# Attention in a macaron block: projections moved to nearly every second step, copies of turned blocks all on ScalarE

## The chip, the cores and the metric

The kernel runs on one core of a Trainium2 chip. The metric is the device time of one execution in microseconds (us). The core has TensorE (PE in the profile; its weight loads are the row PEld), VectorE (DVE), ScalarE (ACT), GpSimd (POOL) and SyncE (SP), which issues the DMAs. Each engine runs its own instructions in order and waits on semaphores for the others.

## What is computed

The block is half a gated feed-forward layer, an attention layer, and the half feed-forward layer again, each on the normalised input and added to it. There are 8 batch items of 512 tokens, width 512, 16 heads of 32 that share one key and one value head.

```
x = x + 0.5 * ffn(layernorm(x))       # silu(x wg) * (x wu), 2 of 4 kept, times wd
x = x + attn(layernorm(x))
x = x + 0.5 * ffn(layernorm(x))

attn: q = x wq', k, v = split(x wkv')        # rotary with xpos scales on q and k
      a = softmax(where(causal, -max, q k' / 32))
      out = (a v) wproj' + b
```

All of it is float32; a product of two float32 matrices is made of three products of rounded parts (high by high, low by high, high by low).

## The kernel before, and what sets the order of its work

The two feed-forward phases take about 1,080 us each; nothing of the change lies in them. Between them stands the attention phase, written by hand: `attention_phase` gives each engine a function `step(K)`, and the order of the calls in it is the order in which the engine works. There are 8 batches (B = 0 to 7) of 16 steps (k = 0 to 15), 128 steps K in all. Four steps make a group: one group of 4 heads, one tile of 128 queries in each step. `ORDER = (3, 0, 1, 2)` says that the first step of a group handles the long row (512 keys), and the next three handle rows of 128, 256 and 384 keys.

**What TensorE does in step K.** It turns (transposes) the probabilities of row K into one PSUM bank for each block of 128 keys (`turn_probs`, L1236): none for the long row, which goes through DRAM, and 1, 2 and 3 blocks for the others. It does the projection that a table sets at this step (`project`): 12 matmuls of 128x512 for keys and values (L1179), for the queries of a group of heads of the next batch (L1204), or for the output of 128 tokens of the batch before (L1267). In the fourth step of a group it turns the inverse sums (L1212), in some steps a normalised tile (L344). In the first step of a group it weighs the values for the group before (`weigh`, 80 small matmuls, L1255). Last it computes the scores of row K+3 into banks 0 to 3 (`scores`, L1227). There is one set of score banks, so these scores wait until VectorE has masked all four heads of row K+2.

**What VectorE does in step K.** It masks the four heads of row K+2 and finds their maxima (`mask_scores`, L1496), after the scores of step K-1. In the fourth step of a group it turns the long row in 32x32 blocks, in two halves (L1506). Then come smaller things: the second block of the row of 384 is copied from PSUM (L1510), a query projection is split (`split_q`, L1479 and L1482), an output tile is added (`add_output`, L1528), the sums are inverted (L1516), the weighed values are scaled (`scale_output`, L1523; it waits for `weigh`), and for the batch after next come statistics (L262), aggregate (L268), the normalised tile (L275) and the rotated keys (`keys`, L1444 to L1470).

**What ScalarE does.** It makes the exponentials of rows K+1 and K+2 (L1367), the other copies of turned blocks (L1372), and single copies of other PSUM banks. Turned blocks, projections, normalised tiles and sums share three PSUM banks in rotation, each of which is taken again when what was put there three turns ago is drained. GpSimd finishes queries, parts outputs, and widens the inverse sums (L1091), which TensorE needs before it turns them.

In the first batch and in the last one other tables (`FIRST_PROJECT`, `LAST_PROJECT`) set the projections: 5 and 4 of them where the six middle batches have 9. In this text T4 (for instance) is the moment at which the scores at the end of TensorE's step k = 4 begin, and "step k = 4 lasts" means from T3 to T4.

Of the kernel before, what the change touches and what calls it, by code (L numbers as in the profile page):

```python
# [26 lines left out]
P = 128  # L27
# [4 lines left out]
def macaron_kernel(nc, x_in, w_gu, w_d, w_q, w_kv, w_p, b_p, rotary_q, rotary_k, out):  # L32
# [140 lines left out]
    with ExitStack() as ctx:  # L173
# [66 lines left out]
        pt_scalar = sem("pt_scalar")  # L240
        pt_vector = sem("pt_vector")
# [646 lines left out]
        def attention_phase(src, dst, m0):  # L888
# [18 lines left out]
            ON_VECTOR = ((), (), (1,))  # L907
            probs_of = (probs0, probs1, probs2)
            TURN_X, TURN_KV, KEYS, TURN_K = {11: 0, 12: 1, 13: 2, 14: 3}, 1, 8, 10
            KEYS_AND_QUERIES = {0: ("kv", 0), 1: ("q", 0), 2: ("q", 1), 5: ("q", 2), 6: ("q", 3)}  # L910
            OUTPUTS = {9: ("out", 0), 10: ("out", 1), 13: ("out", 2), 14: ("out", 3)}
            FIRST_PROJECT = {0: ("kv", 0), 2: ("q", 0), 5: ("q", 1), 6: ("q", 2), 10: ("q", 3)}
            LAST_PROJECT = {2: ("out", 0), 6: ("out", 1), 10: ("out", 2), 14: ("out", 3)}
            STATS = {3: 0, 4: 1, 5: 2, 7: 3}
# [36 lines left out]
            def blocks_before(K, of):  # L951

                one = [sum(1 for j in range(blocks_of(i)) if of(i, j)) for i in ORDER]
                return K // TT * sum(one) + sum(one[:K % TT])

            def turned_by(K, j):
                return blocks_before(K, lambda i, j: True) + j + 1

            def by_vector(i, j):
                return j in ON_VECTOR[i]  # L960

            def by_scalar(i, j):
                return j not in ON_VECTOR[i]

            def copies_of(K, j):

                i = row_of(K)
                mine = by_vector if by_vector(i, j) else by_scalar
                return (pt_vector if mine is by_vector else pt_scalar,
                        blocks_before(K, mine) + sum(1 for n in range(j + 1) if mine(i, n)))  # L970
# [34 lines left out]
            def sync(sp):  # L1005
# [39 lines left out]
                load(3)  # L1045
                for B in range(BATCHES):
                    for hg in range(NHG):
                        turn_long(B * NHG + hg)
                        if B == BATCHES - 1 and hg == 0:
# [104 lines left out]
            def tensor(pe):  # L1154
# [76 lines left out]
                def turn_probs(K, j):  # L1231
                    if j == 0:
                        pe.wait_ge(exp_done, (K + 1) * HG)
                    ps = take_turn(("p", K, j), *copies_of(K, j))
# [4 lines left out]
                def weigh(G):  # L1239
# [8 lines left out]
                    for i in ORDER:  # L1248
                        if i == ORDER[1]:
                            pe.wait_ge(pt_scalar, blocks_before(K, by_scalar))  # L1250
                            pe.wait_ge(pt_vector, blocks_before(K, by_vector))
# [87 lines left out]
            def scalar(a):  # L1339
# [30 lines left out]
                def copy_turned(K, j):  # L1370
                    a.wait_ge(p_turned, turned_by(K, j))
                    a.copy(pt[:, PLACES[row_of(K)][j]], bank_of["p", K, j][:, :].rearrange("p (s n) -> p s n", n=P)).then_inc(pt_scalar, 1)  # L1372
# [16 lines left out]
                def step(K):  # L1389
                    B, k = divmod(K, UNITS)  # L1390
                    nxt = B + 1
                    mine = [j for j in range(blocks_of(row_of(K))) if by_scalar(row_of(K), j)]
# [321 lines left out]
```

## Time and profile before

| | us |
|---|---|
| median of three runs | 2708.21 |
| lowest and highest | 2704.32, 2709.27 |
| the profiled execution | 2706.47 |
| its span | 2704.7 |
| TensorE busy | 2631.6 (97%) |
| VectorE busy | 1882.8 (70%) |
| ScalarE busy | 1100.8 (41%) |
| GpSimd busy | 306.1 (11%) |

Times in the rows below count from the start of the span. A row of a timeline has the start, the duration, the engine, the line of the program with the operation, what it writes and reads, how many instructions the row stands for, and in brackets the idle time of the engine before it with what ended it. The start of the next row is often earlier than the end of this one, since the engines are pipelined; what one instruction costs its engine is the distance of the starts. A row of a table of stretches has the stretch, its length, the busy time and the instructions (x) of TensorE, its weight loads, VectorE, ScalarE and GpSimd, then TensorE's granted clock as a share of the full one, the busy share of the DMA engines, and GB/s.

### The profile page before, as it was taken

The page shows a single profiled execution, that of the slowest core. Times are in us where ns is not written, and L with a number is a line of the kernel's source. Part 1 is how long each engine was busy: PE and PEld are TensorE (multiplying, and loading weights), DVE is VectorE, ACT ScalarE, POOL GpSimd, SP SyncE. Part 2 cuts the span into 40 slices and gives each one's busy share as a digit, 9 for nine tenths or more (in the row PEclk, how much of TensorE's full clock was granted, in tenths as well). Part 3 has the DMA queues.
Part 4 walks back from the last instruction along what each step waited for, and adds up shares of the span by engine and source line. Part 5 has one row for each costly group of instructions (what it writes and reads, how often), then busy time and mean ns, then how long its engine had stood idle before and what let it go on. Part 6 is the DMA issues. An engine that isn't in the chain of part 4 may idle for free.

```text
span 2704.7 us, 40331 instructions
## 1 busy us (share of the span) xinstructions
PE 2631.6 (97%) x14816; PEld 2120.4 (78%) x14816; DVE 1882.8 (70%) x3506; ACT 1100.8 (41%) x2344; POOL 306.1 (11%) x318
## 2 busy tenths in 40 slices
PE   8999999999999999789999989999999999999999
PEld 6888888888888888566666667888888888888887
DVE  6667766765686667778777775657766776677665
ACT  4333333333333332677777773333333333323332
POOL 0000000000000003454455420000000000000000
PEclk9999999999999999899999989999999999999999
DMA  4211411241132111445555553212321141123100
GB/s 143 85 52 53 166 47 47 79 141 47 47 125 94 47 47 43 139 122 153 155 157 157 156 173 125 86 51 78 113 86 58 58 158 61 47 63 125 47 16 32
DMA packets 181224, 248.68 MB, mean 92 GB/s; under 512 B 10304, under 2 KB 100672, under 8 KB 180800
## 3 DMA queue, kind: packets, MB, share of 16 engines
q1 hardware_dynamic: 181056, 246.46, 28.9%
q8 instruction: 104, 1.70, 0.3%
q14 instruction: 64, 0.52, 0.1%
HBM read 175.11 MB, written 71.30 MB: 91 GB/s over the span
## 4 chain that ended last, share of the span: by engine, by line
PE 90%; DVE 6%; ACT 2%; issue 1%; DMA 1%; POOL 0%; SPq 0%; DVEq 0%; POOLq 0%; ACTq 0%
PE bank L466 51%; PE bank L487 25%; PE bank L1204 3%; PE bank L1267 3%; PE bank L1227 3%; PE bank L1236 2%; DVE probs L1496 2%; DVE probs L1506 2%; PE bank L1255 1%; PE bank L1179 1%; PE bank L344 1%; ACT probs L1367 1%; ACT pt L1372 0%; DVE stats L262 0%; PE bank L503 0%
## 5 line engine op out<-in xcount | busy, mean ns | idle before, releaser
L466 PE MATMUL bank<-xnt_h,wgu_h 128*128 128x512 f32 x2048 | 798.9, 390 | 4.2 <-ACT sg L584 2.8
L466 PE MATMUL bank<-xnt_l,wgu_h 128*128 128x512 f32 x2048 | 797.5, 389 | 0.0
L466 PE MATMUL bank<-xnt_h,wgu_l 128*128 128x512 f32 x2048 | 797.4, 389 | 0.0
L659 DVE TENSOR_TENSOR h<-bank,sg 128x512 f32<-128x512 f32 x256 | 176.7, 690 | 538.9 <-PE bank L466 525.2
L466 PEld LDWEIGHTS bank<-xnt_h,wgu_h 128*128 128x128 f32 x2048 | 384.9, 188 | 85.6 <-ACT sg L584 3.7
L466 PEld LDWEIGHTS bank<-xnt_h,wgu_l 128*128 128x128 f32 x2048 | 384.9, 188 | 80.3
L466 PEld LDWEIGHTS bank<-xnt_l,wgu_h 128*128 128x128 f32 x2048 | 384.9, 188 | 79.4
L588 ACT ACTIVATE mag<-h 128x512 f32<-128x512 f32 x256 | 162.0, 633 | 673.2 <-DVE h L659 673.2
L487 PE MATMUL bank<-wd_h,hs_h 128*128 128x512 f32 x1008 | 392.2, 389 | 0.0
L487 PE MATMUL bank<-wd_h,hs_l 128*128 128x512 f32 x1008 | 392.1, 389 | 0.0
L487 PE MATMUL bank<-wd_l,hs_h 128*128 128x512 f32 x1008 | 392.1, 389 | 0.0
L598 ACT CAST hs_h<-h 128x512 fp32r<-128x512 f32 x256 | 155.4, 622 | 567.3 <-DVE h L688 559.8
L1367 ACT ACTIVATE probs<-probs,nmax 128x256 f32<-128x256 f32 (+3 forms) x512 | 284.7, 561 | 26.2 <-DVE nmax L1496 26.2
L1496 DVE CUSTOM_DVE_ANT_0 probs<-bank,causal 128x256 f32<-128x256 f32 (+3 forms) x512 | 218.5, 482 | 21.5 <-PE bank L1227 13.9
L584 ACT ACTIVATE sg<-bank 128x512 f32<-128x512 f32 x256 | 152.5, 596 | 171.9 <-PE bank L466 171.6
L487 PEld LDWEIGHTS bank<-wd_h,hs_l 128*128 128x128 f32 x1008 | 189.2, 188 | 39.3
L487 PEld LDWEIGHTS bank<-wd_l,hs_h 128*128 128x128 f32 x1008 | 189.2, 188 | 39.2
L487 PEld LDWEIGHTS bank<-wd_h,hs_h 128*128 128x128 f32 x1008 | 189.2, 188 | 39.2
L353 POOL TENSOR_SCALAR var_eps<-meanvar 128x4 f32<-128x4 f32 x23 | 6.1, 267 | 1750.3 <-DVE meanvar L268 1750.3
L646 DVE SCALAR_TENSOR_TENSOR x_sb<-bank,x_sb 128x512 f32<-128x512 f32 (+1 forms) x256 | 159.1, 682 | 11.1 <-PE bank L487 5.8
L639 DVE TENSOR_TENSOR wgu_l<-raw_gu,wgu_h 128x1024 fp32r<-128x1024 f32 x124 | 151.0, 1218 | 13.9 <-ACT wgu_h L572 12.7
L694 DVE TENSOR_TENSOR hs_l<-h,hs_h 128x512 fp32r<-128x512 f32 x252 | 156.7, 683 | 0.0
(138 smaller groups left out, 3082.3 us busy)
## 6 DMA issues: line engine op xcount, KB each, us to landing
raw_gu<-in_w_gu SPq DMA_DIRECT2D x128, 512.0 KB, 5.0
raw_d<-in_w_d SPq DMA_DIRECT2D x128, 256.0 KB, 2.6
squares<-probs SPq DMA_DIRECT2D x128, 256.0 KB, 4.1
pt<-squares SPq DMA_DIRECT2D x32, 1024.0 KB, 5.5
x_mid<-x_sb SPq DMA_DIRECT2D x64, 256.0 KB, 2.7
x_squares<-xs SPq DMA_DIRECT2D x48, 256.0 KB, 4.2
xs<-x_squares SPq DMA_DIRECT2D x12, 1024.0 KB, 5.5
x_sb<-x_mid SPq DMA_DIRECT2D x10, 1024.0 KB, 5.9
```

Source lines behind the costliest of these rows:

```text
L466: last = pe.matmul(ps, w[:, r, kind, k], xs[:, b, k], start=(i == 0), stop=(i == 3 * KD - 1))
L487: last = pe.matmul(bank[DOWN + t][:, :], hs[:, b, r, tok], w[:, r], start=(i == 0), stop=(i == 3 * NR - 1))
L584: a.activation(sg[:, r % 2], bank[GATE + r % 2][:, :], ACT.Silu).then_inc(silu_done, 1)
L588: a.activation(mag[:, r], h[:, r], ACT.Abs).then_inc(mag_done, 1)
L598: a.copy(tiles_of(hs_h[:, b, r]), from_quarters(h[:, r])).then_inc(hs_h_done, 1)
L639: v.tensor_tensor(wgu_l[:, r], raw_gu[:, r], wgu_h[:, r].bitcast(F32), ALU.subtract).then_inc(wgu_done, 1)
L646: v.scalar_tensor_tensor(out=x, in0=bank[banks + t][:, :], scalar=0.5, in1=x, op0=ALU.mult, op1=ALU.add).then_inc(added, 1)
L659: v.tensor_tensor(h[:, r], bank[UP + r % 2][:, :], sg[:, r % 2], ALU.mult).then_inc(h_done, 1)
L694: v.tensor_tensor(tiles_of(hs_l[:, b, r]), from_quarters(h[:, r]), tiles_of(hs_h[:, b, r]).bitcast(F32), ALU.subtract).then_inc(hs_done, 1)
L1204: last = pe.matmul(ps[:, :], w[:, k, cols], x[:, 0, k], start=(k == n == 0), stop=(k == KD - 1 and n == 2))
L1367: a.activation(row, row, ACT.Exp, bias=nmax[:, i, s:s + 1], scale=-1.0, accum_out=sums[:, G % 2, s, i:i + 1]).then_inc(exp_done, 1)
L1496: v.tensor_tensor_reduce(out=row_of_head(K, s), in0=scored, in1=mask, scale=1.0, scalar=MASKED, op0=ALU.add, op1=ALU.min, accum_out=nmax[: ...
```

## The change

Four things are changed, all in the attention phase.

1. In the middle batches the projections stand in steps 0, 2, 4, 6, 8 (keys and values, four of queries) and 10, 12, 13, 14 (outputs), and no longer in 0, 1, 2, 5, 6 and 9, 10, 13, 14.
2. ScalarE copies all turned blocks; VectorE's copy (L1510) goes, and one semaphore counts all copies.
3. VectorE's small work is moved: statistics in steps 2, 5, 6, 9 instead of 3, 4, 5, 7; keys in step 9 instead of 8; tiles normalised in steps 10 (two), 12 and 13 instead of 10 to 13; and within a step `drain_projection` and the inversion now come behind the scaled output, the statistics, the keys and the normalised tile, where they stood ahead of them. The turning of a normalised tile moves from step 11 to step 10 for the first tile.
4. The load of the fourth batch item is issued two groups later.

```
-            TURN_X, TURN_KV, KEYS, TURN_K = {11: 0, 12: 1, 13: 2, 14: 3}, 1, 8, 10
-            KEYS_AND_QUERIES = {0: ("kv", 0), 1: ("q", 0), 2: ("q", 1), 5: ("q", 2), 6: ("q", 3)}
+            TURN_X, TURN_KV, KEYS, TURN_K = {10: 0, 12: 1, 13: 2, 14: 3}, 1, 9, 10
+            KEYS_AND_QUERIES = {0: ("kv", 0), 2: ("q", 0), 4: ("q", 1), 6: ("q", 2), 8: ("q", 3)}
...
     def step(K):                                     # ScalarE
...
-                    if 1 in mine:
-                        copy_turned(K, 1)
-                    if 2 in mine:
-                        copy_turned(K, 2)
+                    for j in range(1, blocks):
+                        copy_turned(K, j)
...
     def step(K):                                     # VectorE
                     mask_scores(K + AHEAD - 1, range(HG))
                     if k % TT == TT - 1:
                         turn_squares(K + 1, 0)
-                    if 1 in mine:
-                        copy_turned(K, 1)
-                    if k % TT == TT - 1:
                         turn_squares(K + 1, 1)
-                    if nxt < BATCHES and k == KEYS:
-                        keys(nxt)
-                    drain_projection(B, k)
-                    if k % TT == TT - 2:
-                        invert_sums(K // TT)
                     if k % TT == 0 and K > 0:
                         scale_output(K // TT - 1)
                     if k in STATS:
                         stat(nxt + 1, STATS[k])
-                    if k == 8:
+                    if k == LAST_STAT:
                         ln_aggregate(v, nxt + 1 + m0, slot_of(nxt + 1))
-                    if k + 1 in TURN_X and (nxt < BATCHES or TURN_X[k + 1] < 2):
-                        normalise(nxt + 1, TURN_X[k + 1])
+                    if nxt < BATCHES and k == KEYS:
+                        keys(nxt)
+                    for t in NORMALISE.get(k, ()):
+                        if nxt < BATCHES or t < 2:
+                            normalise(nxt + 1, t)
+                    drain_projection(B, k)
+                    if k % TT == TT - 2:
+                        invert_sums(K // TT)
```

TensorE in a middle batch, from the scores at the end of step 4 to those of step 5, before (kt,qt are the scores, probs the turned blocks, wq a projection of queries, of whose twelve matmuls three rows stand here):

```order
L1255 MATMUL bank<-pt,kvtok 32x128 x24
L1227 MATMUL bank<-kt,qt 128x384 x4
L1236 MATMUL bank<-ident,probs_110 128x128 x4
L1204 MATMUL bank<-xnt_h,wq_h 128x512
L1204 MATMUL bank<-xnt_h,wq_l 128x512
L1204 MATMUL bank<-xnt_l,wq_h 128x512
...
L1227 MATMUL bank<-kt,qt 128x512 x4
```

The same place in the changed kernel, from the last matmuls of the projection that now stands in step 4:

```order
L1194 MATMUL bank<-xnt_l,wq_h 128x512
L1244 MATMUL bank<-pt_108,kvtok 32x128 x16
L1244 MATMUL bank<-pt,kvtok 32x128 x24
L1217 MATMUL bank<-kt,qt 128x384 x4
L1226 MATMUL bank<-ident,probs_110 128x128 x4
L1217 MATMUL bank<-kt,qt 128x512 x4
L1226 MATMUL bank<-ident,probs_92 128x128 x8
```

The projection has moved from behind the scores of 384 to ahead of the weighing, and between the two sets of scores stand four transposes.

VectorE from the masks of the row of 256 keys (step 4) to those of the row of 384 (step 5), before (att is the scaled output, stats the statistics, qt and qtmp the split projection):

```order
L1496 ISA probs_92,nmax<-bank,causal 128x256 [waits score_done]
...
L1523 TENSOR_TENSOR att<-bank,rt 128x512 [waits att_l_done,rt_done,pv_done]
L262 BN_STATS stats<-x_sb 128x6
L1496 ISA probs_109,nmax<-bank,causal 128x384 [waits score_done]
...
L1479 TENSOR_TENSOR qt<-bank,rot_q 128x512 [waits q_done]
L1482 STREAM_SHUFFLE qtmp<-bank 128x512 [waits q_finished]
```

The same place in the changed kernel:

```order
L1483 ISA probs_92,nmax<-bank,causal 128x256 [waits score_done]
...
L1506 TENSOR_TENSOR att<-bank,rt 128x512 [waits att_l_done,rt_done,pv_done]
L1466 TENSOR_TENSOR qt<-bank,rot_q 128x512 [waits q_done]
L1469 STREAM_SHUFFLE qtmp<-bank 128x512 [waits q_finished]
L1483 ISA probs_109,nmax<-bank,causal 128x384 [waits score_done]
...
L261 BN_STATS stats<-x_sb 128x6
```

The split of the projection (qt, qtmp) now stands behind the scaled output and ahead of the masks of 384; the statistics stand behind them.

VectorE in step 9 and the start of step 10, from the end of the masks of 384, in the changed kernel (krot and kwide are the keys, xn a normalised tile, x_sb<-x_sb,bank an added output):

```order
L261 BN_STATS stats<-x_sb 128x6
L267 BN_AGGR meanvar<-stats 128x2 [waits ln_stat]
L1431 TENSOR_TENSOR krot<-kvtok,rot_k 128x128 [waits kvtok_done]
...
L1457 COPY kwide<-krot 128x512 [waits k_step,k_turned]
L1483 ISA probs_107,nmax<-bank,causal 128x16x32 [waits squares_stored,score_done]
...
L274 TENSOR_SCALAR xn<-x_sb,meanvar,rstd 128x512 [waits xn_turned,rstd_step,ln_stat]
L274 TENSOR_SCALAR xn<-x_sb,meanvar,rstd 128x512 [waits xn_turned]
L1511 TENSOR_TENSOR x_sb<-x_sb,bank 128x512 [waits x_biased,proj_done]
```

Before, the keys stood ahead of the masks of 384, in step 8, and only the added output stood between the masks of 384 and those of the long row.

## Rows read from the trace of the kernel before

**Rows 1.** Table of stretches: the first, a middle and the last batch of attention.

```profile
1081.30:1148.90 67.60, 53.60 (x540) 36.37 (x540) 53.52 (x170) 46.34 (x145) 33.14 (x33) 0.90 0.47 137
1286.50:1355.80 69.30, 64.80 (x696) 46.78 (x692) 55.09 (x181) 51.74 (x159) 34.29 (x34) 1.00 0.51 153
1576.20:1640.00 63.80, 52.03 (x595) 37.88 (x595) 46.02 (x149) 47.82 (x149) 11.94 (x15) 0.89 0.55 162
```

**Rows 2.** Timeline of TensorE in a middle batch, steps 0 to 4.

```profile
1299.03 0.71 PE L1227 MATMUL bank<-kt,qt 32*128 32x256 f32 x8
...
1302.71 2.39 PE L1255 MATMUL bank<-pt,kvtok 128*32 128x128 f32 x80
1305.03 0.93 PE L1227 MATMUL bank<-kt,qt 32*128 32x384 f32 x8
...
1306.30 0.47 PE L1204 MATMUL bank<-xnt_h,wq_h 128*128 128x512 f32 x1
...
1309.24 0.46 PE L1187 MATMUL bank<-ident,kvt 64*128 64x64 f32 x4
1309.62 1.14 PE L1227 MATMUL bank<-kt,qt 32*128 32x512 f32 x8
...
1317.39 0.71 PE L1227 MATMUL bank<-kt,qt 32*128 32x256 f32 x8
1318.03 2.39 PE L1255 MATMUL bank<-pt,kvtok 128*32 128x128 f32 x80
1321.74 0.93 PE L1227 MATMUL bank<-kt,qt 32*128 32x384 f32 x8 [1.32 <-DVE nmax L1496]
```

**Rows 3.** Timeline of VectorE in the same steps.

```profile
1305.17 0.69 DVE L1523 TENSOR_TENSOR att<-bank,rt 128x512 f32<-128x512 f32 x1 [2.98 <-PE bank L1255]
1306.02 0.56 DVE L1496 CUSTOM_DVE_ANT_0 probs<-bank,causal 128x384 f32<-128x384 f32 x1 [0.17 <-PE bank L1227]
...
1307.46 0.55 DVE L1496 CUSTOM_DVE_ANT_0 probs<-bank,causal 128x384 f32<-128x384 f32 x1
...
1314.59 0.69 DVE L1479 TENSOR_TENSOR qt<-bank,rot_q 128x512 f32<-128x512 f32 x1 [1.23 <-PE bank L1204]
...
1315.84 0.23 DVE L1516 RECIPROCAL rsum<-sums 128x16 f32<-128x16 f32 x1
...
1316.78 1.24 DVE L1506 STREAM_TRANSPOSE probs<-probs 128x1024 f32<-128x1024 f32 x1
1317.94 0.65 DVE L1510 COPY pt<-bank 128x512 f32<-128x512 f32 x1
...
1319.66 0.65 DVE L262 BATCH_NORM_STATS2 stats<-x_sb 128x6 f32<-128x512 f32 x1
...
1321.26 0.42 DVE L1496 CUSTOM_DVE_ANT_0 probs<-bank,causal 128x256 f32<-128x256 f32 x1
```

**Rows 4.** Timeline of TensorE in the first batch: scores at T8, T9, T10, a tile.

```profile
1126.46 0.93 PE L1227 MATMUL bank<-kt,qt 32*128 32x384 f32 x8 [1.32 <-DVE nmax L1496]
...
1132.44 2.09 PE L1227 MATMUL bank<-kt,qt 32*128 32x512 f32 x8 [4.47 <-DVE nmax L1496]
...
1140.17 0.50 PE L1227 MATMUL bank<-kt,qt 32*128 32x128 f32 x8
...
1144.33 0.66 PE L344 MATMUL bank<-ident,xn 128*128 128x128 f32 x4 [1.45 <-DVE pt L1510]
```

**Rows 5.** Timeline of VectorE in a middle batch, the keys and the scaled output.

```profile
1337.91 0.49 DVE L1444 TENSOR_TENSOR krot<-kvtok,rot_k 128x128 f32<-128x128 f32 x1
...
1339.43 0.68 DVE L1523 TENSOR_TENSOR att<-bank,rt 128x512 f32<-128x512 f32 x1
```

**Rows 6.** Table of stretches: two at a lower granted clock.

```profile
1130.80:1137.70 6.90, 5.26 (x20) 3.50 (x21) 4.02 (x16) 4.00 (x11) 2.90 (x4) 0.51 0.49 152
...
1591.60:1595.10 3.50, 3.50 (x36) 2.40 (x38) 3.50 (x5) 3.32 (x13) 0.00 (x0) 0.51 0.89 359
```

**Rows 7.** Timeline of TensorE in the last batch, ahead of the second such stretch.

```profile
1590.00 0.50 PE L1227 MATMUL bank<-kt,qt 32*128 32x128 f32 x8 [2.50 <-DVE nmax L1496]
```

More of the change, by code:

```diff
@@ L239, in macaron_kernel @@
         pt3_loaded = sem("pt3_loaded")
-        pt_scalar = sem("pt_scalar")
-        pt_vector = sem("pt_vector")
+        pt_copied = sem("pt_copied")
         pv_done = sem("pv_done")
@@ L906, in attention_phase @@
             PLACES = ((0,), (1, 2), (3, 4, 5))
-            ON_VECTOR = ((), (), (1,))
             probs_of = (probs0, probs1, probs2)
-            TURN_X, TURN_KV, KEYS, TURN_K = {11: 0, 12: 1, 13: 2, 14: 3}, 1, 8, 10
-            KEYS_AND_QUERIES = {0: ("kv", 0), 1: ("q", 0), 2: ("q", 1), 5: ("q", 2), 6: ("q", 3)}
-            OUTPUTS = {9: ("out", 0), 10: ("out", 1), 13: ("out", 2), 14: ("out", 3)}
+            TURN_X, TURN_KV, KEYS, TURN_K = {10: 0, 12: 1, 13: 2, 14: 3}, 1, 9, 10
+            KEYS_AND_QUERIES = {0: ("kv", 0), 2: ("q", 0), 4: ("q", 1), 6: ("q", 2), 8: ("q", 3)}
+            OUTPUTS = {10: ("out", 0), 12: ("out", 1), 13: ("out", 2), 14: ("out", 3)}
             FIRST_PROJECT = {0: ("kv", 0), 2: ("q", 0), 5: ("q", 1), 6: ("q", 2), 10: ("q", 3)}
             LAST_PROJECT = {2: ("out", 0), 6: ("out", 1), 10: ("out", 2), 14: ("out", 3)}
-            STATS = {3: 0, 4: 1, 5: 2, 7: 3}
+            STATS, LAST_STAT, NORMALISE = {2: 0, 5: 1, 6: 2, 9: 3}, 9, {10: (0, 1), 12: (2,), 13: (3,)}
             CUT_NEXT = {4: 0, 8: 1}
@@ L949, in in_pieces, with blocks_before @@
                 return ap.rearrange("p (c n) -> p c n", n=32)
-            def blocks_before(K, of):
-                one = [sum(1 for j in range(blocks_of(i)) if of(i, j)) for i in ORDER]
+            def blocks_before(K):
+                one = [blocks_of(i) for i in ORDER]
                 return K // TT * sum(one) + sum(one[:K % TT])
             def turned_by(K, j):
[L957 to L963, printed above, removed]
+                return blocks_before(K) + j + 1
             def copies_of(K, j):
[L967 to L970, printed above, removed]
+                return blocks_before(K) + j + 1
             bank_of = {}
@@ L1044, in sync @@
                 load(2)
-                load(3)
                 for B in range(BATCHES):
@@ L1048, in sync @@
                         turn_long(B * NHG + hg)
+                        if B == 0 and hg == 1:
+                            load(3)
                         if B == BATCHES - 1 and hg == 0:
@@ L1233, in turn_probs @@
                         pe.wait_ge(exp_done, (K + 1) * HG)
[L1234 removed]
+                    ps = take_turn(("p", K, j), pt_copied, copies_of(K, j))
                     for s in range(HG):
@@ L1371, in copy_turned @@
                     a.wait_ge(p_turned, turned_by(K, j))
-                    a.copy(pt[:, PLACES[row_of(K)][j]], bank_of["p", K, j][:, :].rearrange("p (s n) -> p s n", n=P)).then_inc(pt_scalar, 1)
+                    a.copy(pt[:, PLACES[row_of(K)][j]], bank_of["p", K, j][:, :].rearrange("p (s n) -> p s n", n=P)).then_inc(pt_copied, 1)
                 def drain_sums(G):
@@ L1391, in step @@
                     nxt = B + 1
-                    mine = [j for j in range(blocks_of(row_of(K))) if by_scalar(row_of(K), j)]
+                    blocks = blocks_of(row_of(K))
                     if nxt < BATCHES:
@@ L1554, in step @@
                     B, k = divmod(K, UNITS)
-                    i, nxt = row_of(K), B + 1
-                    mine = () if i == LONG else ON_VECTOR[i]
+                    nxt = B + 1
                     mask_scores(K + AHEAD - 1, range(HG))
```

8 lines of the change are left out of this document (2 added, 6 removed).

## The prediction, made before the changed kernel ran

> **What bounds the kernel now.** I read the table of stretches first, since the page's shares mix three phases. The feed-forward phases are TensorE's without a hole and the change does not touch them. Only the 559 us of attention can move. In a middle batch TensorE is busy 64.8 of 69.3 us, VectorE 55.1, ScalarE 51.7 [rows 1]. So a middle batch is 64.8 us of TensorE's work plus 4.5 us in which it waits, and there are six such batches. All that even projections can win there is 6 x 4.5 = 27 us. The first and the last batch have fewer projections: TensorE is busy only 53.6 of 67.6 and 52.0 of 63.8 us [rows 1]; they are bound by the chain scores, masks, scores.
>
> Next I read the timeline of TensorE by steps. From T to T: step 0 lasts 6.00 us (1299.03 to 1305.03), step 1 4.59, steps 2 and 3 together 7.77, step 4 4.35 [rows 2]. Only the last shows a large wait, 1.32 us for VectorE's masks (nmax). It comes back in step 8. The timeline of VectorE tells why: behind the masks of 128 come two turnings of the long row, a copy between them, a statistic, and only then the masks of 256, whose last ends at 1321.26 + 0.42 = 1321.68; TensorE goes on 0.06 us later [rows 2, 3]. So step 4, without a projection, is VectorE's; the steps with one are TensorE's.
>
> **Prices.** A projection takes 1309.24 - 1306.30 = 2.94 us of TensorE. The weighing takes 2.32 (1302.71 to 1305.03). Scores of 384 and four transposes take 1.27 (1305.03 to 1306.30), the turning of the values 0.38 [rows 2]. On VectorE, counted from T0: the scaled output starts at +0.14, since it waits for the weighing, and the masks of 384 at +0.99, since they wait for their scores (the bracket says L1227). The first to the last of the four masks is 1.44, the last takes 0.55, and TensorE follows 0.06 later. A split projection takes 1315.84 - 1314.59 = 1.25, by the distance of starts [rows 3]. Where no next start stands in the rows I take the duration less an overlap of some 0.08: the turning of 1.24 is followed by the copy after 1.16. That gives 0.57 for the copy (0.65), 0.57 for a statistic and 0.61 for the scaled output (0.69).
>
> **Part 1, the projections of a middle batch.** The work of TensorE stays the same, so I count waits.
>
> Steps 4 and 8 now hold a projection. TensorE's work there is 0.64 + 2.32 + 2.94 = 5.9, taken as 6.0 like step 0. VectorE needs 4.35 in such a step before, and less now. The waits of 1.32 go, twice a batch: -2.6 us.
>
> Steps 5 and 9 lose theirs. TensorE has 1.27 us of work between T4 and the scores of the long row, and then needs the four masks of 384 done. VectorE has the scaled output from +0.14, then, by the new order, the split of the projection from +0.75 to +2.00, then the masks: +2.00 + 1.44 + 0.55 + 0.06 = 4.05. The wait is 4.05 - 1.27 = 2.8 us, twice a batch: +5.6. The query projection has long been done by then, but VectorE stands at the scaled output, waiting for the weighing, with the split queued behind it. Who waits for that is TensorE.
>
> Step 1 loses its projection too. The keys' and values' projection is drained by ScalarE, so the masks start at +0.99 and T1 = T0 + 0.99 + 1.44 + 0.55 + 0.06 = 3.04 against 1.27 + 0.38 = 1.65 of work: a wait of 1.4.
>
> Steps 2, 3, 6, 7 have the same work and the same chain from the split over the inverse sums as before. Step 10: VectorE has statistic, aggregate and keys between the masks of 384 and of 512. The keys are 1.52 us there (1337.91 to 1339.43) [rows 5]. In the first batch T8 to T9 was 5.98 [rows 4]; less the scaled output and the masks (0.61 + 2.05) this leaves at most 3.3 for them. With 1.52 the long row's masks end about 4.7 us behind T9 and the first normalised tile at 5.2, an estimate; TensorE is ready at about 4.9 and waits some 0.4 for it. Steps 11 and 13 wait for a bank: the copy of the tile 0.3; in step 13 the output of step 12 is added only after the scaled output and a tile, at about T12 + 1.9, where TensorE wants the bank at +1.27, 0.6. Small waits that stay, about 0.15 each in three steps: 0.4.
>
> The waits come to 5.6 + 1.4 + 0.4 + 0.3 + 0.6 + 0.4 = 8.7 us against 4.5 now. That is **+4.2 us a batch, +25.2 for six**. From below: if the split cost nothing in steps 5 and 9, they would be 3.04 like step 1, and the batch +2.2. From above: keys at 3.3 us in each batch add 1.8: +6.0.
>
> **Part 2, the copies.** One instruction of 0.65 us a group leaves VectorE and goes to ScalarE, 32 in all; of its 0.57 nothing is on the path in a middle batch now, since the projection in steps 4 and 8 covers it. ScalarE is busy 51.7 of 69.3 us and takes 2.6 more. Queued behind the copy there are the exponentials of the next row, which TensorE needs a step later. I take 0; if it delayed the weighing, 0 to 0.3 in each group that has no projection in its first step.
>
> In the first batch the steps 4 and 8 still have no projection. There the copy (0.57) and the statistic (0.57) leave the path: -1.15 with the overlaps, twice. Floor: TensorE's 0.64 + 2.32 = 2.96, against 4.35 - 1.15 = 3.20, so nothing new binds.
>
> By the Trainium skill (Perfetto Trace Analysis, Optimizing Scalar/DVE Operations) work should go to ScalarE if VectorE is saturated. VectorE is busy 79% in the batch, and ScalarE 75%, so by that rule the two terms of 1.15 would be nothing. The wait of 1.32 says that VectorE is late in one step while idle in others, so I keep them.
>
> **Part 3, small work in the first and last batch.** In the first batch the keys stood in step 8 ahead of the masks of 384, and TensorE waited 4.47 us: T8 to T9 is 5.98 [rows 4]. Now nothing stands there but the scaled output: 3.04, which is -2.9. The clock then fell to the lower level (1.2 GHz; granted 0.51) from 1130.8 to 1137.7 [rows 6], and T9 to T10 was 7.73. With the keys now between, it may be 6.4 to 7.9; I take 7.0, -0.7. The tile that waited 1.45 us for VectorE's copy in step 11 [rows 4] is turned a step earlier: -1.5. First batch: -2.3 - 2.9 - 0.7 - 1.5 = **-7.4**. Last batch: projections and their order stay (all in the third step of a group, where no scaled output precedes them); three copies and some statistics leave the first steps of groups: **-2**, from -4 to +2. The later load takes DMA time away from the first group, where the masks of 512 are not the last to wait: 0.
>
> **The sum without the clock.** 2706.5 (the profiled execution, span 2704.7) + 25.2 - 7.4 - 2 = 2722.3.
>
> **The clock.** The granted clock fell behind the waits of 4.47 and 2.50 us [rows 4, 6, 7] and never in the middle batches, where the longest wait is 1.32. The new waits of 2.77 lie above 2.50, and around them stand scores and transposes as there. There are 12. I take a fall behind 8 of them. A fall that lasts 3.5 us at half clock, as the second one [rows 6], with a projection in it, costs half of that, 1.7; the first one held TensorE's work from 1132.44 to 1137.7 [rows 4, 6], half of which is 2.6. So +13.6, from 0 to 12 x 2.6 = 31. Sum: 2735.9. The median of three runs lies 1.7 above the profiled execution, so I say 2737.6, rounded to **2737**.
>
> The Trainium skill (Perfetto Trace Analysis, Matmul Optimizations) says that the matmul engine scales its power with utilization, so that matmuls should be executed in batches, back to back. That speaks against spreading the projections. By it the sum is the one with falls, without it 2724. The rows of the first and last batch agree.
>
> **Rivals.**
> Slower, clock full: the masks of 384 hold steps 1, 5 and 9 as worked out, and the clock holds as it does behind the waits of 1.32: 2722.3 + 1.7 = 2724.
> No change: VectorE's split runs beside the scores in steps 5 and 9, the end of +2.2: 13.2 - 9.4 = +3.8, so 2712. Against it stands the order: the split is queued behind the scaled output, whose wait ended at T0 + 0.14 in the trace.
> Faster: the waits in steps 5 and 9 do not arise at all, because the weighing there ends early and VectorE finds its masks' scores before TensorE runs out of other work. The middle batch would keep 1.4 + 1.8 = 3.2 of waits, -1.3, and with the two end batches 6 x -1.3 - 9.4 = -17: 2691. It decides from +1.6 a batch downwards (9.4 / 6). Against it: TensorE has 1.27 us of work there, and the masks alone take 2.05.
> That the change does not do what it says is out: the order of instructions shows the projections moved.
>
> **How the numbers follow.** Slower with falls of the clock 0.55; slower at full clock 0.30; no change 0.07; faster 0.08. The range: the unknown costs of keys (up to +11) and of the clock (0 to 31; all of both at once I leave out) upwards, the end batches +-4, and down to the edge of the second case: 2712 to 2754. A difference of 0.2% is about what can be told from none here. Faster by more 0.08, within 0.07, slower 0.85.
>
> **What would show it.** Middle batches of 73.5 us, or 75.5 with the clock; waits of about 2.8 us of the scores of 512 (L1217 by the new line numbers) for VectorE twice a batch and 1.4 once; none of 1.32 ahead of the scores of 384; VectorE's split starting 0.7 us behind the weighing; a clock below 1.00 in middle batches; a first batch of about 59. I am wrong if the scores of 512 in steps 5 and 9 follow their transposes at once, or if the clock shows 1.00 in all middle batches.

## The result

The changed kernel takes 2738.13 us (median of 4 runs, 2733.45 to 2745.18), the kernel before 2707.93 in the same session: a ratio of 1.0117, with a 95% interval of 1.0100 to 1.0134. It is slower by 1.2%. The profiled execution of it took 2738.21 us, its span is 2736.2, 31.5 us above the span before (2704.7).

The table of stretches of the changed kernel, with the columns of [rows 1]: the first batch, the six middle batches together, one middle batch, the last batch with what stands behind it, and three short stretches inside the middle batch. The first and the last stretch have other bounds than those of [rows 1] and are not to be compared with them by their length; from the first scores to T12 the first batch lasts 63.8 us, where it lasted 67.5.

```profile
1087.90:1157.40 69.50, 57.81 (x568) 40.03 (x568) 56.43 (x184) 52.49 (x163) 36.24 (x38) 0.90 0.48 147
1157.40:1618.10 460.70, 413.44 (x4153) 295.73 (x4152) 325.01 (x1062) 319.52 (x980) 203.81 (x205) 0.95 0.46 136
1309.50:1384.90 75.40, 67.16 (x693) 48.06 (x692) 54.07 (x178) 53.20 (x164) 33.97 (x35) 0.98 0.49 141
1618.10:1680.00 61.90, 54.78 (x700) 40.74 (x700) 44.77 (x146) 51.73 (x157) 12.48 (x15) 1.00 0.69 219
1333.40:1336.80 3.40, 0.81 (x11) 0.34 (x8) 3.27 (x12) 2.91 (x9) 3.24 (x4) 1.00 0.36 63
1336.80:1340.30 3.50, 3.50 (x19) 2.48 (x12) 2.56 (x9) 1.52 (x4) 0.74 (x1) 0.51 0.66 255
1340.30:1343.70 3.40, 3.40 (x25) 2.60 (x24) 1.52 (x4) 2.27 (x7) 0.00 (x0) 1.00 0.00 0
```

The six middle batches of the kernel before, in the same view:

```profile
1160.60:1576.20 415.60, 388.69 (x4153) 280.64 (x4152) 329.99 (x1085) 310.34 (x955) 205.30 (x205) 1.00 0.51 151
```

The six take 45.1 us more for the same 4153 rows of matmuls, and the granted clock is 0.95 where it was 1.00. TensorE is busier by 24.8 us with the same work, for the most part because matmuls at the lower level of the clock last longer. Next to nothing outside attention moved: its first scores begin 0.6 us later, and what follows the last T12 takes 1073.6 us in both. Measured from T15 to T15, the first batch ended 3.1 us earlier, the middle batches took 45.0 us more, and the last batch, from there to its T12, 10.3 us less. 45.0 - 3.1 - 10.3 = 31.6, within 0.1 of the difference of the spans.

TensorE in steps 4 to 6 of that middle batch, to be laid beside [rows 2]:

```profile
1326.21 0.71 PE L1217 MATMUL bank<-kt,qt 32*128 32x256 f32 x8
...
1329.80 2.39 PE L1244 MATMUL bank<-pt,kvtok 128*32 128x128 f32 x80
1332.12 0.93 PE L1217 MATMUL bank<-kt,qt 32*128 32x384 f32 x8
1332.97 0.66 PE L1226 MATMUL bank<-ident,probs 128*128 128x128 f32 x4
1336.22 1.48 PE L1217 MATMUL bank<-kt,qt 32*128 32x512 f32 x8 [2.58 <-DVE nmax L1483]
1337.63 1.97 PE L1226 MATMUL bank<-ident,probs 128*128 128x128 f32 x8
...
1342.65 0.50 PE L1217 MATMUL bank<-kt,qt 32*128 32x128 f32 x8
```

VectorE in the same steps, beside [rows 3]:

```profile
1328.89 0.42 DVE L1483 CUSTOM_DVE_ANT_0 probs<-bank,causal 128x256 f32<-128x256 f32 x1
...
1332.25 0.69 DVE L1506 TENSOR_TENSOR att<-bank,rt 128x512 f32<-128x512 f32 x1 [2.94 <-PE bank L1244]
1332.86 0.68 DVE L1466 TENSOR_TENSOR qt<-bank,rot_q 128x512 f32<-128x512 f32 x1
1333.47 0.73 DVE L1469 STREAM_SHUFFLE qtmp<-bank 128x512 f32<-128x512 f32 x1
1334.09 0.54 DVE L1483 CUSTOM_DVE_ANT_0 probs<-bank,causal 128x384 f32<-128x384 f32 x1
...
1335.51 0.55 DVE L1483 CUSTOM_DVE_ANT_0 probs<-bank,causal 128x384 f32<-128x384 f32 x1
```

Read them together. Step 4 lasts 5.91 us (1326.21 to 1332.12): the wait of 1.32 is gone. But the projection it holds was finished at about 1329.8, and its split begins at 1332.86, behind the scaled output, which waits 2.94 us for the weighing. The masks of 384 thus begin at 1334.09, 1.97 us after their scores began, and the scores of the long row wait 2.58 us for them. The transposes behind that wait then run at the lower level of the clock: 1.97 us for eight where 1.10 is usual, and step 6 lasts 6.44 instead of 4.85.

The longest waits of this middle batch and of one of the kernel before show the exchange; first the changed kernel (columns: who waits for whom, us in total, times, the longest):

```profile
DVE att L1506 <- PE bank L1244: 13.1, 4, 3.9
...
PE bank L1217 <- DVE nmax L1483: 6.4, 3, 2.6
```

and the kernel before:

```profile
DVE att L1523 <- PE bank L1255: 4.8, 2, 3.0
...
PE bank L1227 <- DVE nmax L1496: 2.6, 2, 1.3
```

VectorE now stands still for the weighing four times a batch instead of twice, and TensorE stands still for the masks for 6.4 us of a batch instead of 2.6.

### The profile page after: what moved, and what is told of

It is laid out like the page before. It is cut to its first block, busy times and chain, and to the rows that moved or that the text cites. A ratio compares the mean times of both kernels' runs of the same rounds, so it can differ in the third digit from the quotient of the medians.

```text
span 2736.2 us, 40299 instructions
## 1 busy us (share of the span) xinstructions
PE 2651.3 (97%) x14816; PEld 2132.5 (78%) x14816; DVE 1874.1 (68%) x3474; ACT 1113.2 (41%) x2376; POOL 305.1 (11%) x318
## 4 chain that ended last, share of the span: by engine, by line
PE 90%; DVE 5%; issue 1%; ACT 1%; POOL 1%; DMA 0%; SPq 0%; DVEq 0%; POOLq 0%; ACTq 0%
PE bank L465 50%; PE bank L486 25%; PE bank L1194 3%; PE bank L1256 3%; PE bank L1217 2%; PE bank L1244 2%; DVE probs L1483 2%; PE bank L1226 2%; PE bank L1169 1%; PE bank L343 1%; DVE qtmp L1469 1%; PE bank L1202 1%; ACT probs L1356 0%; DVE att L1506 0%; PE bank L502 0%
## 5 line engine op out<-in xcount | busy, mean ns | idle before, releaser
L1217 PE MATMUL bank<-kt,qt 32*128 32x512 f32 (+3 forms) x1024 | 111.9, 507 | 50.8 <-DVE nmax L1483 50.3
```

The costliest lines, as they stand in the source:

```text
L1217: last = pe.matmul(bank[SCORES + s][:, 0:width(i)], qt[rows, B % 2, hg, i * P:(i + 1) * P], kt[rows, B % 2, 0:width(i)], start=True, stop= ...
```

## The experiments

Each kernel was timed beside the kernel before, and its ratio is to that one in the same session. Step times are distances of T's in a middle batch, without a fall of the clock unless said. "The six batches" are counted from the T15 of the first batch on.

| kernel | median us | ratio to before, 95% | six middle batches, us |
|---|---|---|---|
| before | 2707.93 | 1 | 415.7 |
| the change | 2738.13 | 1.0117 (1.0100 to 1.0134) | 460.7 |
| e1: small drains first | 2720.31 | 1.0051 (1.0034 to 1.0067) | 443.3 |
| e2: old places | 2672.82 | 0.9880 (0.9864 to 0.9897) | 396.2 |
| e3: new places alone | 2731.19 | 1.0092 (1.0075 to 1.0109) | 445.8 |
| e4: matmuls in the waits | 2722.27 | 1.0060 (1.0043 to 1.0076) | 443.5 |
| e5: copies alone | 2693.29 | 0.9960 (0.9946 to 0.9974) | 409.6 |
| e6: small work alone | 2684.95 | 0.9925 (0.9908 to 0.9941) | 402.4 |
| e7: all query splits first | 2723.47 | 1.0061 (1.0044 to 1.0078) | 446.5 |
| e8: places and copies | 2712.85 | 1.0027 (1.0018 to 1.0037) | 430.1 |
| e9: two splits first | 2716.59 | 1.0044 (1.0027 to 1.0061) | 437.8 |
| e10: e2 with the early load | 2675.63 | 0.9895 (0.9879 to 0.9912) | 396.0 |

### Is it the split behind the scaled output?

e1, an edit of the changed kernel, in VectorE's step:

```
+                    drain_projection(B, k)
+                    if k % TT == TT - 2:
+                        invert_sums(K // TT)
                     if k % TT == 0 and K > 0:
                         scale_output(K // TT - 1)
...
-                    drain_projection(B, k)
-                    if k % TT == TT - 2:
-                        invert_sums(K // TT)
```

> The changed kernel with one thing undone: within a step of VectorE the split of a projection (and the inverted sums) stands ahead of the scaled output again. Theory (queue order): in steps 5 and 9 of a middle batch the masks of 384 start 1.0 us earlier, those steps fall from 4.10 to 3.1 us and step 13 from 5.3 to 4.7, the wait of the scores of 512 from 2.6 to 1.6 us; the falls of the clock behind them go, which cost 17.7 us. Sum: 2738 - 12 - 4 - 18 = 2705. Rival (only the place of the projections matters, not the queue): 2738. Rival (waits of 1.6 still bring the clock down): 2722.

Measured 2720.31, against the change 0.7% less and 15 us more than my theory said. The steps in dispute did what it said: steps 5 and 9 last 3.14 us instead of 4.10. What was not expected stands in step 10. TensorE there, and VectorE:

```profile
1351.80 1.14 PE L1217 MATMUL bank<-kt,qt 32*128 32x512 f32 x8 [1.62 <-DVE nmax L1483]
...
1358.91 0.63 PE L343 MATMUL bank<-ident,xn 128*128 128x128 f32 x4 [2.19 <-DVE xn L274]
```

```profile
1352.88 1.31 DVE L1432 TENSOR_TENSOR krot<-kvtok,rot_k 128x64 f32<-128x64 f32 x1
...
1357.55 0.68 DVE L1511 TENSOR_TENSOR x_sb<-x_sb,bank 128x512 f32<-128x512 f32 x1
1358.15 0.24 DVE L1499 RECIPROCAL rsum<-sums 128x16 f32<-128x16 f32 x1
1358.31 1.20 DVE L274 TENSOR_SCALAR xn<-x_sb,meanvar,rstd 128x512 f32<-128x512 f32 x2
```

Step 10 lasts 8.11 where the change had 6.64, for two reasons. The added output and the inversion (L1511, L1499) now stand ahead of the normalised tile that TensorE turns in step 10, some 0.7 us. And the rotated keys take 2.40 us instead of 1.62, since one of their operations (L1432) falls beside a GpSimd operation, 0.8 us; e9 below has this second part alone. The clock fell behind four of the six waits of 2.19 and behind none of the twelve of 1.62. So 2720 is near the number of the second rival (2722), but not for its reason: the edit took one cause away and made another.

e9 moves the split of steps 4 and 8 alone, in the middle batches; e7 the splits of all query steps. Both are edits of the changed kernel, in the same place (the comments are added here):

```
+                    split_here = 0 < B < BATCHES - 1 and k in (4, 8)      # e9
+                    split_here = k in queries_in(B)                       # e7
+                    if split_here:
+                        drain_projection(B, k)
                     if k % TT == 0 and K > 0:
                         scale_output(K // TT - 1)
...
-                    drain_projection(B, k)
+                    if not split_here:
+                        drain_projection(B, k)
```

> The changed kernel with only two splits a middle batch, those of steps 4 and 8, put ahead of the scaled output. Theory: steps 5 and 9 fall from 4.10 to 3.14, steps 3 and 7 stay at 2.9 (no statistic between split and inverted sums), step 10 gives 0.8 back because the keys now meet GpSimd's work; one or two falls of the clock left. Sum: 2738 - 11.5 + 4.7 - 17.7 + 3 = 2716.5. Rival (nothing is given back in step 10): 2712. Rival (the falls stay): 2731.

> The changed kernel with only the split of query projections put ahead of the scaled output; output tiles are added where the change has them. Theory: steps 5 and 9 fall from 4.10 to 3.14, step 10 stays at 6.6 (no wait of 2.2 as in the kernel that put all drains first), waits of 1.6 us behind which the clock stays. Sum: 2738 - 11.5 - 17.7 = 2709. Rival (waits of 1.6 twice a batch bring falls too): about 2722.

e9 came to 2716.59 with a forecast of 2716.5: steps 5 and 9 at 3.14, and step 10 at 7.42 (+0.8: step 9 ends 1 us earlier there, and the keys now meet GpSimd's work and take 2.40 us). The clock fell twice in the six batches: once behind a wait of 1.62, where it cost nothing (step 10 waits for VectorE either way), and once in step 0 of the first of them, behind no wait above 1.3, where it cost 1.5 us. e7 missed its forecast by 14 us. It has the same step 10 as e9 (7.43), for which the forecast had 6.6. In steps 2 and 6 of the change the statistic fills the time in which the split waits for its projection; in e7 it comes behind the split, and the inversion of the sums behind both. What TensorE turns of the sums in steps 3 and 7 is late, and these steps last 3.50 instead of 2.90. Together they say: the split's place behind the scaled output costs just under 1 us in each of steps 5 and 9, and most of the falls with it; each of the three orders lost something elsewhere, and none is faster than the kernel before.

### How much of it is the clock?

e4 leaves VectorE's order alone and gives TensorE eight matmuls of 128x512, read by nobody, in steps 5 and 9 of the middle batches:

```
+                    if 0 < B < BATCHES - 1 and k in (5, 9):
+                        pe.wait_ge(att_done, K // TT)
+                        for n in range(8):
+                            pe.matmul(outs[:, :], wq_h[:, n % KD, 0:P], xnt_h[:, 0, n % KD], start=True, stop=True)
```

> The changed kernel with eight added matmuls of 128x512 on TensorE in the wait of steps 5 and 9 of the middle batches, into the bank of the weighed values, which are already read; their result is not used. They take about 1.9 of the 2.6 us of the wait. Theory (waits bring the clock down, falls cost 17.7 us in all): steps 5 and 9 stay at 4.1 us, no fall in a middle batch, steps 6 and 10 at 4.9 and 6.6 each time. Sum: 2738 - 18 = 2720. Rival (the falls come from elsewhere, the long wait is all that costs): 2738 or more.

TensorE in e4, steps 5 and 6:

```profile
1328.34 0.93 PE L1217 MATMUL bank<-kt,qt 32*128 32x384 f32 x8
...
1329.61 2.08 PE L1294 MATMUL bank<-xnt_h,wq_h 128*128 128x512 f32 x8
1332.45 1.14 PE L1217 MATMUL bank<-kt,qt 32*128 32x512 f32 x8 [0.76 <-DVE nmax L1487]
...
1337.31 0.50 PE L1217 MATMUL bank<-kt,qt 32*128 32x128 f32 x8
```

Step 5 is still 4.11 (1328.34 to 1332.45): the masks set it, not TensorE. Step 6 is 4.86. The table of stretches gives its six middle batches:

```profile
1157.80:1601.30 443.50, 415.74 (x4253) 298.55 (x4252) 325.14 (x1062) 319.62 (x980) 204.25 (x205) 1.00 0.47 141
```

More work, a clock of 1.00 throughout, and 17.2 us less than in the change. In the change the clock fell behind 9 of the 12 waits of 2.58, so a fall costs 17.2 / 9 = 1.9 us. The other 45.0 - 17.2 = 27.8 us are waits. By the Trainium skill (Perfetto Trace Analysis, Matmul Optimizations) the matmul engine scales its power with its use, and matmuls should come back to back. The traces agree: with the waits partly filled the clock is 1.00 over the six batches, without it is 0.95.

### What each part is worth

e3 is the kernel before with only the new tables of projections; e8 adds to it that ScalarE makes all copies; e5 is the kernel before with only that; e6 is the kernel before with only the small work moved, the later load with it. e2 is the changed kernel with the old tables. The edits (the comments are added here; e5 and e8 also drop TensorE's wait for VectorE's copies, and e6's lines are those of points 3 and 4 of the change):

```
+            KEYS_AND_QUERIES = {0: ("kv", 0), 2: ("q", 0), 4: ("q", 1), 6: ("q", 2), 8: ("q", 3)}   # e3, e8
+            OUTPUTS = {10: ("out", 0), 12: ("out", 1), 13: ("out", 2), 14: ("out", 3)}              # e3, e8
+            ON_VECTOR = ((), (), ())                                                                # e5, e8
+            KEYS_AND_QUERIES = {0: ("kv", 0), 1: ("q", 0), 2: ("q", 1), 5: ("q", 2), 6: ("q", 3)}   # e2, to the change
+            OUTPUTS = {9: ("out", 0), 10: ("out", 1), 13: ("out", 2), 14: ("out", 3)}               # e2, to the change
```

> The changed kernel with the projections of the middle batches back in their old steps (0, 1, 2, 5, 6 and 9, 10, 13, 14); copies all on ScalarE and VectorE's small work as changed. Theory: steps 4 and 8 take 3.2 us instead of 4.35 (before), step 10 one more and step 11 one less, no wait above 1.7 us, no fall of the clock in a middle batch. Middle batches 66.8 us against 69.3 before; first and last batch as in the changed kernel (4 and 10 us shorter than before). Sum: 2708 - 15 - 4 - 10 = 2679. Rival (the move of copies and small work is what costs): above 2708.

> The kernel before with the new steps of the projections alone. The split stands ahead of the scaled output, VectorE keeps its copy and its small work. Theory: steps 4 and 8 take 5.9, steps 5 and 9 3.1 and step 1 3.1, middle batches 71.1 against 69.3; first and last batch as before, clock falls there as before and none in the middle. Sum: 2708 + 11 = 2719. Rival (the places alone bring the whole loss, with the clock): 2738. Rival (even places are a gain and the rest spoils it): below 2708.

> The kernel before with one thing changed: ScalarE copies all turned blocks. Theory: VectorE's 0.58 leaves the path in steps 4 and 8 (4.35 to 3.8 each) and the wait of a tile for that copy in step 11 shrinks (4.11 to about 3.5); middle batches 69.3 to 67.5, so -10.6 for six, first batch -2, last batch -2 with the clock's falls there open by 7 either way. Sum: 2706 - 15 = 2691. Rival (the copy was hidden, or ScalarE's exponentials come late for it): 2706 or more.

> The kernel before with VectorE's small work moved as in the change (statistics, keys, normalised tiles, drains behind them; the first tile turned in step 10), but projections in their old steps and the copy still on VectorE. Theory: steps 4 and 8 lose the statistic (4.35 to 3.8), step 11 the tile (4.11 to about 3.2), step 10 gains 0.6: middle batches 67.3, -12 for six; the first batch loses the 4.5 us wait of its step 9, -4; last batch -3 with the falls open. Sum: 2706 - 19 = 2687. Rival (small work behind the scaled output costs): above 2706.

> The kernel before with the new steps of the projections and all copies on ScalarE; small work as before. Theory: in the kernel with the new steps alone the projection of step 4 waited for a bank that VectorE's copy held; now steps 4 and 8 fall from 6.53 to 5.9, steps 5 and 9 to 3.14 with waits of 1.6, step 11 from 4.11 to 3.5: -2.2 a batch, and no falls in middle batches, -9, ends -3. Sum: 2731 - 25 = 2706. Rival (the bank is not what steps 4 and 8 wait for): 2725 or more.

e2 is the fastest kernel of this study, 1.2% below the kernel before (2679 was forecast, 2672.82 measured: steps 9 and 12 are shorter too, 4.19 and 3.55 for 4.39 and 3.96). Its step 8, where the kernel before waited 1.32, shows no wait at all, nor does step 9:

```profile
1321.36 0.71 PE L1217 MATMUL bank<-kt,qt 32*128 32x256 f32 x8
1322.00 2.39 PE L1244 MATMUL bank<-pt,kvtok 128*32 128x128 f32 x80
1324.53 0.93 PE L1217 MATMUL bank<-kt,qt 32*128 32x384 f32 x8
...
1328.72 1.14 PE L1217 MATMUL bank<-kt,qt 32*128 32x512 f32 x8
```

Steps 4 and 8 last 3.17 there (4.35 before): the copy and the statistic have left the stretch ahead of the masks of 256. A middle batch takes 65.7 us, 0.9 above the 64.8 that TensorE is busy [rows 1].

e3 was to be 2719 and came to 2731.19. Here are TensorE's rows for its step 5, and the row of VectorE that stands there between the scaled output and the masks of 384:

```profile
1330.94 0.93 PE L1227 MATMUL bank<-kt,qt 32*128 32x384 f32 x8
...
1334.41 1.14 PE L1227 MATMUL bank<-kt,qt 32*128 32x512 f32 x8 [1.96 <-DVE nmax L1496]
```

```profile
1331.68 0.68 DVE L262 BATCH_NORM_STATS2 stats<-x_sb 128x6 f32<-128x512 f32 x1
```

The forecast left out three things. In steps 4 and 8 the projection first waits some 0.6 us for a bank that VectorE's copy still holds (these steps last 6.53, not 5.9). Steps 5 and 9 wait 1.96 and 1.72 us although the split is ahead of the scaled output, since the old order puts a statistic (step 5) or the aggregate (step 9) behind it, ahead of the masks. And the clock fell six times in the six batches, five of them behind one of these waits. e5, with the copies alone, gains 0.4% (2691 forecast, 2693.29 measured): in steps 4 and 8 the copy is off the path (3.75 for 4.35), of which step 9 gives 0.6 back (5.00 for 4.39), where the keys take 2.14 us instead of 1.53. e6, with the small work alone, gains 0.75% (2687 forecast, 2684.95 measured). e8 is the new places without the held bank: 5.91 in steps 4 and 8, three falls instead of six, and some 18 us less than e3. The forecasts of e3 and e8 (2719 and 2706) both had too few falls, none in the six batches, and steps 5 and 9 too short (3.47 and 3.26 in e8, where 3.14 was expected).

The worth of a part depends on the places of the projections, in one case even its sign. Taking each ratio times 2708:

| | old places | new places |
|---|---|---|
| small work and copies as before | 0 | +25 (e3) |
| copies on ScalarE | -11 (e5) | +7 (e8) |
| small work moved | -20 (e6) | not run |
| copies on ScalarE, small work moved | -32 (e2) | +32 (the change) |

At the old places the parts do add up: -11 and -20 are -31, and both together give -32. The moved small work is worth -21 us on top of the copies there and costs +25 at the new places. In its order a split comes behind the scaled output. At the old places no query projection stands in a step with a scaled output, so the order costs nothing; the new places put two there in every batch. That is most of the +25: e9, which takes only these two splits out of that order, stands at +12, 20 us below the change. What is left to e8 lies in steps 10 and 13 (7.42 and 5.34 for 5.30 and 4.63), against which steps 5, 9 and 11 together give 1.1 back.

e10 is e2 with the load of the fourth item at the start again:

```
                 load(2)
+                load(3)
...
-                        if B == 0 and hg == 1:
-                            load(3)
```

> The changed kernel with the old steps of the projections (2673 us), and the load of the fourth batch item back at the start of attention. Theory (that load is hidden either way): 2673, within 0.2%. Rival (it delays the first long row by DMA): 1 to 3 us slower, all of it in the first batch.

2675.63, with an interval of the ratio (0.9879 to 0.9912) that overlaps with that of e2 (0.9864 to 0.9897): what the place of the load is worth can't be told from nothing.

## Why the prediction was right, and where it was not

It said 2737 and slower, with waits of the masks and a clock that falls; measured were 2738.13 and both of these. Three of its small numbers do not follow from its own terms: 2737.6 rounds to 2738, a middle batch with the clock is 73.5 + 13.6 / 6 = 75.8 and not 75.5, and the first batch would be 67.6 - 7.4 = 60.2 and not 59. By its own steps:

**Steps 4 and 8** were to take 5.9 to 6.0 and take 5.91 and 5.93; the waits of 1.32 are gone. **Steps 5 and 9** were to take 4.05 and take 4.10, with waits of 2.58 (2.8 forecast), for the reason given: the split starts 0.61 us behind the scaled output's start (0.61 was its price), not when its projection ends. e9 shows it: with this split alone moved, 3.14 us. **Step 1** was to take 3.04 and takes 3.14. That difference is in one term: TensorE goes on 0.06 us behind the end of the masks of 256 [rows 2, 3], and I took that for the long row too, where it is 0.16 (1335.51 + 0.55 = 1336.06, to 1336.22).

**Step 10** was to wait some 0.4 us for the first normalised tile; the wait is 0.73. Here are the rows of the changed kernel, VectorE's keys and then TensorE's turning:

```profile
1356.49 0.57 DVE L1431 TENSOR_TENSOR krot<-kvtok,rot_k 128x128 f32<-128x128 f32 x1
1356.99 0.21 DVE L1432 TENSOR_TENSOR krot<-kvtok,rot_k 128x64 f32<-128x64 f32 x1
...
1361.24 0.63 PE L343 MATMUL bank<-ident,xn 128*128 128x128 f32 x4 [0.73 <-DVE xn L274]
```

**Step 13** takes 5.34 us, and 4.63 in e1, where the added output stands ahead of the scaled one: 0.7 for a forecast of 0.6. In all a middle batch without a fall takes 73.9 us (read from e4, since each of the six has a fall in the change), where 69.3 + 4.2 = 73.5 was forecast: +4.6 for +4.2. Over six batches the waits came to 27.8 us for a forecast of 25.2.

**The clock** fell behind 9 of 12 waits (8 forecast), at 1.9 us each (1.7 forecast): 17.2 for 13.6. Both were near, but they were guesses. The 1.7 was for falls of 3.5 us, and five of the nine lasted 6.8. The count went by the waits of 4.47 and 2.50 alone, and that was a misreading of the trace of the kernel before: its last batch shows two more falls, at waits of 1.97 and 1.62, and its first scores one behind a wait of 1.75. Here is the wait of 1.97 and the stretch behind it:

```profile
1600.35 1.14 PE L1227 MATMUL bank<-kt,qt 32*128 32x512 f32 x8 [1.97 <-DVE nmax L1496]
```

```profile
1601.80:1605.30 3.50, 3.50 (x13) 3.00 (x12) 2.57 (x9) 3.10 (x9) 0.00 (x0) 0.51 0.62 207
```

Read so, the kernel before already spoke more strongly against the rival of a full clock, and against forecasts of no fall behind 1.6 to 2 us (e3, e8). The runs fill this in. In the middle batches the clock fell, in the stretch at or just behind a wait, in this share of the cases:

| wait of TensorE, us | kernel | falls of waits |
|---|---|---|
| 1.24 | the change, e1, e3, e4, e7, e8, e9 | 2 of 42 (e3, e7) |
| 1.32 | before | 0 of 12 |
| 1.50 | e7, e9 (the tile of step 10) | 0 of 12 |
| 1.62 | e1, e7, e9 | 0, 1, 1 of 12 each |
| 1.68 to 1.75 | e3, e8 | 2 of 12 |
| 1.96 | e3, e8 | 6 of 12 |
| 2.19 | e1 | 4 of 6 |
| 2.58 | the change | 9 of 12 |

What decides between two waits of the same length in one kernel stays open. The table leaves out falls around the start of the first middle batch, which e1, e2, e5, e7, e9 and e10 have and the others have not: they stand behind several waits of up to 1.3 us at the end of the first batch and cost some 1.5 us, in e1 2.6. So the length of the last wait is not all that counts.

**The first batch** was to gain 7.4 us and gained 3.1. (From the first scores on it gained 3.8.) Three terms held: steps 4 and 8 take 3.17 each (3.20 forecast), step 9 takes 3.14 (3.04). Two failed. Step 11 was to take 1.5 less and takes 4.35 for 4.74, only 0.4 less, since the lower clock reaches into it. The larger one is step 10, "7.0", from 6.4 to 7.9: it takes 9.65. Its rows, TensorE first, then VectorE, then GpSimd:

```profile
1128.11 1.14 PE L1217 MATMUL bank<-kt,qt 32*128 32x512 f32 x8 [1.63 <-DVE nmax L1483]
...
1135.89 1.09 PE L343 MATMUL bank<-ident,xn 128*128 128x128 f32 x4 [2.87 <-DVE xn L274]
```

```profile
1129.26 1.07 DVE L1431 TENSOR_TENSOR krot<-kvtok,rot_k 128x128 f32<-128x128 f32 x1
...
1131.05 1.27 DVE L1453 TENSOR_TENSOR krot<-krot 128x128 f32<-128x128 f32 x1
```

```profile
1128.90 1.27 POOL L1075 TENSOR_TENSOR wp_l<-raw_p,wp_h 128x512 fp32r<-128x512 f32 x1
...
1130.88 1.28 POOL L1089 TENSOR_TENSOR att_l<-att,att_h 128x512 fp32r<-128x512 f32 x1
```

The rotated keys fell beside GpSimd's work here and took 3.50 us for 1.62 in a middle batch, so the tile came late, TensorE waited 2.87 us for it, and the clock fell again: L343 takes 1.09 us here for 0.63 in a middle batch. Of the 9.65 us, 6.64 are what step 10 takes in a middle batch, 1.9 the longer keys, 0.9 the lower clock, and 0.2 a longer aggregate. The fall of the kernel before was not removed but moved one step on. I had listed the keys' spread (1.52 to 3.3 us) and not asked what a late tile would do to the clock.

**The last batch** was to gain 2 us, from -4 to +2, and gained 10.3: outside its bounds. VectorE of the kernel before waits 4.98 us there for the DMA that brings the long row back, and the clock fell three times; in the changed kernel it waits 2.90, and the clock stays at 1.00. The rows of VectorE, the kernel before and the changed one:

```profile
1587.41 0.69 DVE L1496 CUSTOM_DVE_ANT_0 probs<-bank,causal 128x512 f32<-128x512 f32 x1 [4.98 <-DMA squares<-probs]
```

```profile
1626.98 0.69 DVE L1483 CUSTOM_DVE_ANT_0 probs<-bank,causal 128x512 f32<-128x512 f32 x1 [2.90 <-DMA squares<-probs]
```

Most of this is probably not the change's doing. e3 has the code of the kernel before in its last batch and took 47.7 us for the stretch in which before took 54.8 and the change 44.5. So some 7 of the 10.3 come with another alignment of the DMA and of the falls (e5, likewise with old small work, took 46.6), and some 3 may go to the copies and the small work, near the 2 forecast; since the other kernels show 44.4 to 49.9 for this stretch, from one trace each, this division is argued, not shown. I took one execution's last batch for what the code gives there. The two misses, +4.3 in the first batch and -8.3 in the last, together with +6.2 in the middle, come to +2.2: part of the closeness of 2737 to 2738 is misses that cancel.

**The copies** at 0 in the middle batches were right for the change, where the projection covers them, and **the load** at 0 too (e10). But the price belongs to the surroundings: at the old places the copies alone gain 11 us (e5), and at the new ones 18 (e8 less e3), because VectorE's copy held the bank that the projection needed.

**The rivals.** Full clock (2724) is what e4 gives, whose clock holds in the middle batches: 2722.27, with the same misses in its end batches. The nine falls alone decided against it. No change (2712) is the kernel in which the split does not wait behind the scaled output: e9, 2716.59, with 3.14 in steps 5 and 9 (3.04 by its words), above it by about what the 0.8 in step 10 comes to in six batches. Faster (2691) needed steps 5 and 9 without a wait; even in e9 they wait 1.6.

## What to carry to other kernels

When work is spread evenly over an engine, look at what drains it on the next engine, and at what stands ahead of that drain in its queue: here each projection was early, and its split stood behind an operation that waits for later work. Price two edits of one schedule together, since the same reordering gained 21 us at one set of places and cost 25 at the other; of a change with several parts, try the parts that move least first (e2 keeps the old tables and beats both). A wait of some 2 us on TensorE may cost as much again by the clock; work that nobody reads, put into it, shows how much.

## What the runs showed of the hardware

A VectorE operation on two small tensors in SBUF can last six times its time beside a GpSimd operation. In e7, GpSimd:

```profile
1427.06 1.27 POOL L1068 TENSOR_TENSOR qt<-qt,qtmp 128x512 f32<-128x512 f32 x1
```

and VectorE:

```profile
1427.11 1.30 DVE L1432 TENSOR_TENSOR krot<-kvtok,rot_k 128x64 f32<-128x64 f32 x1
```

The same operation takes 0.21 us in the changed kernel at 1356.99, where GpSimd's ended at about that time. It seems to wait until GpSimd's is over, rather than to share with it: it ends at 1428.41 and GpSimd's at 1428.33, and GpSimd's takes no longer than its usual 1.27 us. The Trainium skill (GPSIMD Engine Reference, Specifications) says that GpSimd's access to SBUF is shared with VectorE and that VectorE's instructions with two inputs in SBUF contend for it; both inputs of the rotated keys lie there, so the rows agree. That the same operation is 0.21 or 1.30 us by where GpSimd stands is what made step 10 hard to price: its keys take 1.62 us in the middle batches of the change, 2.40 in those of e1, e7 and e9, and 3.50 in the first batch of the change.

The clock was the other surprise: it fell behind waits of 1.96 us in half the cases, of 1.62 in two of 36 and of 1.24 in two of 42, rather than from some length on. In the change a fall of 3.4 or 6.8 us at 0.51 cost 1.9 us on the average, from 0.7 to 2.9 by what stood in it; in e7 and e9 a fall in step 10, where TensorE waits for VectorE anyway, cost nothing (7.42 with it and without).
